# Moving the scaling, rounding and clipping passes of the weight blocks from VectorE to GpSimd in a gated cross-attention and quantised feed-forward block

## What is computed

```python
x = x + tanh(g_xattn) * attention(layernorm(x), ctx, ...)
#   h   = tanh(txt_proj[:, None] + feat_proj[:, :, None] + b)     # for every pair (row, text row): 512 values
#   rho = h @ w ;  att = softmax(rho + mask) ;  then two gates from att @ ctx
x = x + tanh(g_ffn) * ffn(layernorm(x), ...)
#   xq   = fake_quant(x)
#   gate = xq @ wq(w_gate).T ;  up = xq @ wq(w_up).T
#   h    = fake_quant(silu(gate) * up) ;  h @ wq(w_down).T
def wq(w):                                     # weight quantisation, by rows
    scale = max(abs(w), axis=1, keepdims=True) / 127
    return clip(round(w / scale), -128, 127) * scale
```

## Time and profile before

| | us |
|---|---|
| median of 3 runs | 1412.11 (1405.0 to 1412.8) |
| profiled execution, its time | 1408.1 |
| profiled execution, span of the trace | 1406.3 |
| ACT busy | 1260.0 (90%) |
| DVE busy | 1168.8 (83%) |
| PE busy | 1110.7 (79%) |
| POOL busy | 13.9 (1%) |

### The profile page before, as it was taken

One profiled execution on the slowest core, in us unless ns is written; L12 is line 12 of the kernel. 1 busy time (PEld: TensorE's weight loads), 2 busy tenths in 40 slices (PEclk: granted clock), 3 DMA queues, 4 the chain that ended last, 5 costly groups with the idle time before them and its releaser, 6 DMA issues.

```text
span 1406.3 us, 16785 instructions
## 1 busy us (share of the span) xinstructions
PE 1110.7 (79%) x6891; PEld 369.2 (26%) x6891; DVE 1168.8 (83%) x1679; ACT 1260.0 (90%) x481; POOL 13.9 (1%) x32
## 2 busy tenths in 40 slices
PE   6887768778767776679779779787667659999898
PEld 4322112212212221123222122121111115444343
DVE  7688898887899898788978878868899947888777
ACT  3998999899999999999999999999999966666695
POOL 3000000000000000000000000000000000000000
PEclk9998889889998998999999999999998879999999
DMA  6000011100010000000000010000000004411196
GB/s 219 1 15 16 16 45 60 53 23 1 23 38 32 22 24 0 1 1 6 31 21 6 16 43 1 1 0 0 1 1 0 1 16 142 150 52 48 64 346 211
DMA packets 29872, 61.43 MB, mean 44 GB/s; under 512 B 3771, under 2 KB 5835, under 8 KB 29797
## 3 DMA queue, kind: packets, MB, share of 16 engines
q1 hardware_dynamic: 27840, 59.52, 12.7%
q10 hardware_dynamic: 1253, 0.85, 0.2%
q0 software_dynamic: 704, 0.01, 0.0%
HBM read 46.20 MB, written 14.16 MB: 43 GB/s over the span
## 4 chain that ended last, share of the span: by engine, by line
ACT 59%; PE 27%; DVE 13%; issue 1%; DMA 0%; SPq 0%; DVEq 0%
ACT big L491 58%; PE ps L1151 10%; DVE big L681 8%; PE ps L1169 6%; PE ps L971 5%; PE ps L1024 3%; PE ps L1029 1%; DVE bn L616 1%; PE ps L1117 1%; PE ps L1131 0%; DMA wgu<-in_x_dram 0%; DVE big L581 0%; DVE wsc L764 0%; DVE wgu L624 0%; PE ps L961 0%
## 5 line engine op out<-in xcount | busy, mean ns | idle before, releaser
L491 ACT ACTIVATE big<-big 128x6144 f32<-128x6144 f32 (+2 forms) x205 | 1063.6, 5279 | 21.4 <-DVE big L681 21.3
L681 DVE TENSOR_SCALAR big<-big,atxt 128x2048 f32<-128x2048 f32 (+2 forms) x918 | 792.8, 922 | 154.6 <-PE ps L1024 139.5
L1024 PE MATMUL ps<-big,wslide 128*32 128x512 f32 x4312 | 615.1, 643 | 215.3 <-ACT big L491 212.0
L1024 PEld LDWEIGHTS ps<-big,wslide 128*32 128x32 f32 x4312 | 143.3, 114 | 645.0 <-ACT big L491 335.4
L1151 PE MATMUL ps<-aux,wgu 128*128 128x512 bf16 x680 | 151.5, 379 | 0.0
L1029 PE MATMUL ps<-big,wslide 128*32 128x512 f32 x616 | 91.1, 700 | 43.4 <-ACT big L491 43.4
L971 PE MATMUL ps<-big,aux 128*128 128x512 f32 x256 | 118.3, 605 | 2.1 <-ACT big L449 2.1
L536 ACT ACTIVATE aux<-ps,sgux 128x512 f32<-128x512 f32 x88 | 59.9, 686 | 56.8 <-PE ps L1151 55.9
L916 DVE SCALAR_TENSOR_TENSOR big<-ps,sgux,aux 128x512 f32<-128x512 f32 x88 | 65.9, 749 | 25.3 <-PE ps L1151 17.0
L1151 PEld LDWEIGHTS ps<-aux,wgu 128*128 128x128 bf16 x680 | 65.3, 98 | 73.4
L1169 PE MATMUL ps<-wd,wgu 128*128 128x512 bf16 x352 | 78.1, 386 | 3.0 <-DVE wgu L932 3.0
(11 more groups left out here) (153 smaller groups left out, 419.3 us busy)
## 6 DMA issues: line engine op xcount, KB each, us to landing
aux<-in_x_dram SPq DMA_DIRECT2D x96, 256.0 KB, 2.7
out_dram<-aux SPq DMA_DIRECT2D x32, 256.0 KB, 3.6
hidden_spill<-big SPq DMA_DIRECT2D x6, 768.0 KB, 5.5
big<-hidden_spill SPq DMA_DIRECT2D x6, 768.0 KB, 7.3
wgu<-in_x_dram SPq DMA_DIRECT2D x11, 256.0 KB, 7.3
aux<-in_L_ffn_w_gate_dram SPq DMA_DIRECT2D x11, 256.0 KB, 2.6
aux<-in_L_ffn_w_up_dram SPq DMA_DIRECT2D x11, 256.0 KB, 2.9
aux<-in_L_ffn_w_down_dram SPq DMA_DIRECT2D x4, 704.0 KB, 4.0
```

Of the source, the lines that this page charges most:

```text
L491: nc.scalar.activation(unit, unit, ACT.Tanh).then_inc(tanh_done, 1)
L681: v.tensor_scalar(ring[:, place(p)], src, atxt[:, e, bt * T + t:bt * T + t + 1], None, ALU.add).then_inc(sums_ready, 1)
L1024: last = mm(bank(k)[32 * part:32 * part + 32, :], wslide[:, e, 31 - g:63 - g], unit[:, part * 512:(part + 1) * 512], start=(e == 0 and g = ...
```

## The change

The scaling, rounding and clipping passes leave DVE and become a list of their own on POOL (`round_weights`). DVE keeps the row maxima, the two small operations and the move of the scale. POOL waits for the reciprocal (`wt_step`), does the scaling passes, waits for its own writes (`wt_scaled`) and for PE's transposes of the job before (`wq_transposed`), and does the rounding and clipping, which gives `wq_ready` to PE and SP. DVE gets a new wait: it may write the scales of a job only when POOL has done with the job before (`wq_ready`).

The tables are also changed. Jobs 1 to 5 now stand 18 pieces apart, so that the jobs that stood at 96, 112 and 128 stand at 104, 122 and 140; in the second stage the last five stand at 383, 401, 440, 470 and 500 in place of 378, 400, 445, 475 and 522. Jobs 0, 6, 7, 8 and 9 keep their places (50, 200, 220, 262, 365). PE transposes 6 pieces behind the job in place of 1, and the copies move with it.

```diff
-        QUANT_AT = dict(zip((50, 64, 80, 96, 112, 128, 200, 220, 262, 365, 378, 400, 445, 475, 522), range(NJOB)))
-        WT_AT = {at + 1: j for at, j in QUANT_AT.items()}
-        WCOPY_AT = {later(at + 1): j for at, j in QUANT_AT.items()}
+        QUANT_AT = dict(zip((50, 68, 86, 104, 122, 140, 200, 220, 262, 365, 383, 401, 440, 470, 500), range(NJOB)))
+        WT_AT = {at + 6: j for at, j in QUANT_AT.items()}
+        WCOPY_AT = {later(at + 6): j for at, j in QUANT_AT.items()}
...
-        MSTD_AT, SD_AT = 530, 545
+        MSTD_AT, SD_AT = 535, 550
...
+            def round_weights(job):
+                kind, row = JOBS[job]
+                parts, width = (1, I) if kind == "d" else (2, 2 * D)
+                step = width // parts
+                pool.wait_ge(wt_step, 3 * (job + 1))
+                for c in range(parts):
+                    part = wstage[:, c * step:(c + 1) * step]
+                    last = nc.gpsimd.tensor_scalar(part, part, wsc[:, 2 + c:3 + c], MAGIC, ALU.mult, ALU.add)
+                last.then_inc(wt_scaled, 1)
+                pool.wait_ge(wt_scaled, job + 1)
+                if job:
+                    pool.wait_ge(wq_transposed, job)
+                nc.gpsimd.tensor_scalar(wq_sb[:, 0:width], wstage[:, 0:width], MAGIC, QMAX, ALU.subtract, ALU.min)\
+                  .then_inc(wq_ready, 1)
+
+            for job in range(NJOB):
+                round_weights(job)
...
-                lead = 4 * job
-                step = width // parts
+                lead = 3 * job
...
-                def scaled():
-                    for c in range(parts):
-                        part = wstage[:, c * step:(c + 1) * step]
-                        last = v.tensor_scalar(part, part, wsc[:, 2 + c:3 + c], MAGIC, ALU.mult, ALU.add)
-                    return last
-
+                if job:
+                    dve.wait_ge(wq_ready, job)
...
-                        lambda: v.reciprocal(wsc[:, 2:2 + parts], wsc[:, 0:parts]),
-                        scaled)):
+                        lambda: v.reciprocal(wsc[:, 2:2 + parts], wsc[:, 0:parts]))):
...
-                dve.wait_ge(wt_step, lead + 4)
-                if job:
-                    dve.wait_ge(wq_transposed, job)
-                v.tensor_scalar(wq_sb[:, 0:width], whole, MAGIC, QMAX, ALU.subtract, ALU.min).then_inc(wq_ready, 1)
```

More of the change, by code:

```diff
@@ L234, in flamingo_gated_block @@
         wt_step = sem("wt_step")
+        wt_scaled = sem("wt_scaled")
         wq_transposed = sem("wq_transposed")
```

## The result

The changed kernel takes 1413.66 us (median of 20 runs, 1411.39 to 1417.82) against 1407.55 us before (20 runs): a ratio of 1.0049, 95% interval 1.0038 to 1.006. So it is slower by half a per cent, 6 us, where the prediction said 3.4 us faster. 1413.66 lies inside the stated range of 1398 to 1417 and inside "within 1%", but on the other side of the kernel before.

A forecast was written before the change was run, and what follows sets the result against it. ACT was taken as the bound, DVE costing only where ACT waits for adds. Terms -4.17 - 0.9 + 0.6 + 0 + 1.1 = -3.4 us gave 1404.7 (profiled) or 1408.7 (median); forecast 1406, range 1398 to 1417.

The forecast's parts named there:

- within 1%: Whole kernel: time stays within 1% of before, chance 0.83; faster by over 1% 0.07, slower by over 1% 0.10.
- What bounds the kernel: Attention stage: ACT bounds, DVE costs only where ACT waits for adds; 21.3 of 21.4 us idle, a ceiling of 1.5%.
- Jobs 4 and 5 moved away: Jobs at 112 and 128 leave late stretches: the 0.94 wait goes, 3.79 becomes 0.56; gain 4.17 us.
- the rival in which the job at 122 brings a wait back: Job 4's new place: 0.9 to 1.5 of the 4.17 gain goes, sum -2 us; inside the main case's 0.50.
- Job 0: Keeps its place; the add starts at 130.45, behind POOL's first pass, in place of 131.36; gain 0.9 us.
- Jobs 8 and 9: Unmoved jobs: at 8 all three passes push in, loss 0.6 us; at 9 about 1.57 lost and gained, 0.
- The price of a pass on POOL: POOL at a cast's slope, 0.81 ns a column: 0.60, 1.01, 1.32 us for 512, 1024, 1408 columns; "gu" job 2.2.
- The rival with a slower POOL: POOL beyond the double slope, 5.6 us a "gu" job, makes the run slower by over 1%; chance 0.10.
- What a pass takes from DVE: DVE's adds beside POOL: one add between two passes waits for the whole pass, 2.2 us a "gu" job.
- Jobs 10 to 13 hidden by ready units: DVE gives 1.57 us and may lose 2.2; ready units hide it; without that cover, 0.6 each.
- Job 14 at p = 500: Between two adds where DVE waited 2.93 us; POOL's passes run 0.4 and 0.7 over; loss 1.1 us.
- The rival with the double slope: POOL at 3.9 us a "gu" job: sum +4.8 us, 1413 on the profiled execution, 1417 on the median; chance 0.22.

The follow-up runs named there:

- the ten kernels of the table above: The kernel before, the changed kernel and its whole-kernel variants in places, engine or form of passes; ratios to before 0.9921 to 1.0049, ACT's waits 10.0 to 26.6 us.
- the small kernel: Kernel without the computation, timing POOL's passes alone and beside DVE's adds; alone, subtract and minimum took 3.63 us for 1024 and 4.94 for 1408 columns.
- the cheap form: Changed kernel with POOL's second pass as multiply by 1.0 and add minus the constant, without the minimum; ratio to before 0.9964 (0.995 to 0.9978).

## Why the prediction was wrong, step by step

- **What bounds the kernel: right.** The times follow ACT's waits for adds through the ten kernels of the table above.
- **Jobs 4 and 5 moved away: right in the profiled execution, but not in every run.** Forecast 4.17 us, measured 0.94 + 3.79 - 0.40 = 4.33; the run with the long pass cut agrees (0.42 left). But the runs with the down blocks on DVE and with the last five jobs at their old places have the same first ten jobs, and there the waits stay. ACT in the latter:

```profile
243.91 20.98 ACT L509 ACTIVATE big<-big 128x6144 f32<-128x6144 f32 x4 [1.17 <-DVE big L699]
265.17 5.33 ACT L509 ACTIVATE big<-big 128x6144 f32<-128x6144 f32 x1 [0.29 <-DVE big L699]
272.13 31.40 ACT L509 ACTIVATE big<-big 128x6144 f32<-128x6144 f32 x6 [1.63 <-DVE big L699]
```

That is a gain of 1.64, less even than in the rival in which the job at 122 brings a wait back (2.7 to 3.3); job 0 gives more there (2.0). Jobs 0, 4 and 5 together gave 4.8 us in the first two runs (a new wait of 0.5 ahead of job 0 counted) and 3.4 and 3.6 in the others, against a forecast of 5.1. What decides between the two patterns stays open.
- **Job 0: the number right, by luck.** Forecast 0.9, measured 4.52 - 3.53 = 0.99. The 0.9 rested on POOL's first pass going ahead of the add. In the trace the add starts right behind the move, at 132.26, and takes its usual 1.28 us; POOL's pass, from 132.39 on, is the one that waits. DVE reached this add 1.6 us sooner behind its copy than before, the whole of the passes. That ACT got only 0.99 of it is not explained by the block.
- **Jobs 8 and 9: priced too dear, by 0.4 and 1.4 us.** Job 8: forecast a loss of 0.6, measured 0.42 + 1.02 - 1.26 = 0.18. Job 9: forecast 0, measured a gain of 2.23 - 0.57 - 0.29 = 1.37.
- **The price of a pass on POOL: the step that failed first.** The scaling was right (0.69 and 1.44 against 0.60 and 1.32 us). The second pass was taken at the slope of a cast, on the ground that the cast, too, reads, converts and writes; it costs 3.63 and 4.94 us alone in place of 1.01 and 1.32, 3.6 times as much. Even the upper bound, one slope for each arithmetic step, gave only 1.85 and 2.47. The slope was not a property of reading and writing columns but of one form of operation. The rival with a slower POOL had set its mark at 5.6 us a gate-and-up job: alone it is 2 x 0.69 + 3.63 = 5.0.
- **What a pass takes from DVE: right in size for the gate and up blocks, by two errors that cancel.** Forecast: the whole pass, 2.2 us a job. Measured in the small kernel: 0.36 to 0.43 us of each scaling pass (adds of 1.64 and 1.71 in place of 1.28) and 1.56 of the 3.63, 2.3 to 2.4 a job. The pass is dearer than thought, and holds DVE for less than half of it. The Trainium skill (SBUF — State Buffer, "Who interferes with whom") says of a VectorE operation in a two-port mode and a GpSimd instruction that the second to come is fully blocked for the whole instruction. The adds beside 1152 and 1408 columns agree (5.10 and 5.95 us); those beside 1024 columns and less (1.9 and 2.05) do not.
- **Jobs 10 to 13 hidden by ready units: right for job 10, wrong for the down blocks 11 to 13.** The cover was argued for a loss of 2.2 us in pieces. A down block takes 5.3 to 5.8 us from DVE (0.6 to 1.1 for the scaling, 4.7 for the rest, by adds of 1.6 to 2.1 and 5.7 us in place of 1.0), most of it from one add. Jobs 11 to 13 then reached ACT with 6.9 us.
- **Job 14 at p = 500: right place, wrong size.** That POOL would push the adds behind the pair was forecast, at 1.1 us; it was 5.32 - 0.93 = 4.39. The first pass cost 0.3 us, as forecast (0.4); the second cost 4.1 in place of 0.7. With DVE doing the passes at the same place it is 1.78 - 0.93 = 0.85.

Added up: -4.33 - 0.99 + 0.18 - 1.37 + 6.88 + 4.39 = +4.8 us, and with a wait of 0.48 ahead of job 0 that was not there before +5.2, which is the growth of ACT's idle time in the two profiled executions. Without the down blocks' two terms the sum is -6.0. So the sign hung on one unmeasured price, and on a shut-out that the forecast had counted as a sum over passes without asking where a long one falls. That these two terms are the cause is shown by the runs with the down blocks on DVE, with the pass cut, and with the cheap form: each takes the loss away by another door. That the longest single shut-out, and not the sum, is what the ready units cannot cover is argued and not shown, since the cut and the cheap form lower both. The rival with the double slope had +4.8, close to the +6 measured; that is luck, since its sum came from jobs 0, 4, 8, 9 and 14, of which only job 14 paid such a price, and held nothing for jobs 11 to 13.

## What to carry to other kernels

An operation that moves to an engine that has not run it before must be priced by its own form; another operation of the same width is no bound, and two forms of one instruction differed 3.6 times here. Where two engines can shut each other out, compare what a pass keeps out, the longest single one first, with the slack of the instruction that waits at that place: cut in two, the long pass of this case left ACT 16.1 us of waits in place of 26.6. And look first at where a piece of work stands: moving the jobs away from the late stretches gave 0.6% with the work still on the busy engine, and the move to the idle engine gave no more that could be measured.

## What the runs showed of the hardware that was not expected

- On POOL, tensor-scalar with multiply and then add takes 1.36 to 1.44 us for 1408 columns, to f32 and to bf16; all other forms that were tried take 3.77 us with one step (to bf16) and 4.95 with two (subtract and minimum to both types). A cast takes 1.36. The Trainium skill (GPSIMD Engine Reference, "Engine selection") calls one-input operations roughly line-rate; that agrees with the first (0.83 ns a column) and not with the others (3.4 ns for each further column of subtract and minimum).
- A subtract-and-minimum pass of POOL of 512 to 1024 columns let DVE's adds in between and made an add about 0.3 to 0.8 us longer; one of 1152 or 1408 columns kept an add out for 3.8 and 4.7 us. The width at which this turns lies between; its reason stays open. A multiply-and-add pass kept an add out for 0.8 us at 1024 columns and 1.1 at 1408, most of its own 1.1 and 1.4 us.
- The span that the profile gives a POOL pass holds its waits. The same scaling of 512 columns that takes 0.69 us alone stands at job 0 of the changed kernel with 2.82, while two adds went ahead of it at their usual length:

```profile
132.39 2.82 POOL L444 TENSOR_SCALAR aux<-aux,wsc 128x512 f32<-128x512 f32 x1 [114.57 <-DVE wsc L780]
```
